# Reordering the learning step of a two-layer memory and mixture kernel

## The chip, the cores and the metric

The kernel is one program on one core of a Trainium2 chip. The metric is the device time of one execution in microseconds (us), as the median of several runs; one further execution was recorded by the hardware profiler, and its trace is what is read below. The engines are named as in the profile: PE is the matrix engine, PEld its weight loads, DVE the vector engine, ACT the scalar engine, POOL the GpSimd engine and SP the engine that issues DMAs.

## The reference, cut to what matters

The whole program is a chain of five parts on an input of 16 batches of 512 rows with 128 features. The change touches only the first part up to its end: a small memory network (`mem`: two weight matrices `w0`, `w1` and a scale `ln`) that is trained by gradient steps, one after the other, over 8 chunks of 64 rows of all 16 batches.

```python
def mem_fwd(params, x):
    w0, w1, ln = params
    h = jax.nn.silu(x @ w0.T)
    y = h @ w1.T
    return x + rmsnorm(y, ln)
...
k = rmsnorm(jax.nn.silu(xc @ wk_w.T), k_norm_w)
v = jax.nn.silu(xc @ wv_w.T)
...
def step(carry, inp):
    mem, surp = carry
    k_c, v_c, th_c, eta_c, beta_c = inp
    def loss_fn(p):
        pred = mem_fwd(p, k_c)
        return jnp.mean((v_c - pred) ** 2 * th_c[:, :, None])
    grads = jax.grad(loss_fn)(mem)
    total = jnp.sqrt(sum((jnp.sum(g * g) for g in grads)))
    clip = jax.lax.stop_gradient(jnp.minimum(MAX_GRAD_NORM / (total + 1e-06), 1.0))
    new_surp = tuple((eta_c * s_ - g * clip for s_, g in zip(surp, grads)))
    new_mem = tuple((beta_c * m + ns for m, ns in zip(mem, new_surp)))
    return ((new_mem, new_surp), None)
```

Chunk s+1 needs the weights that chunk s leaves, so the 8 steps are serial. Keys, values and the three gates of a chunk do not depend on the weights and are prepared ahead. After the steps come attention, a mixture of experts, a second attention and a second mixture; they are the same in both kernels.

## The kernel before, in words

`learn` is the first part. The 1024 rows of a chunk are held as 8 tiles (`CT`) of 128 rows and 128 features, in two halves of 4 tiles (`HT`), h = 0 and h = 1. Every engine has its own instruction list, written out by hand as a loop `for s in range(NC)` over the 8 steps; the order of the calls in that list is the order of execution on that engine, and semaphores (`Signal`, with `wait_ge` and `then_inc`) tie the lists together. There is no scheduler. One engine's waiting instruction holds up all that stand behind it in its list.

In step s the engines do two things at once.

The training step itself, along the data: PE multiplies keys by `w0` (`hidden`, L437), ACT takes a tanh (L629), DVE makes the hidden values from it (L858), PE transposes them (L451), ACT copies (L637), PE multiplies by `w1` (`output`, L461), ACT squares (L645), DVE sums (L868), POOL takes the root `r` (L768), ACT normalises (`normalise_y`, L651). DVE forms the error and its derivatives (`errors` L874 and L876, `derivatives` L881 to L890), which give per row a number `dr`; ACT multiplies by it (`along_y`, L657), DVE subtracts and so has the gradient `dy` of a half (`remainder`, L895). PE transposes it (`transpose_dy`, L469), ACT copies the transpose (`copy_dyt`, L667), PE sends it back through `w1` (`grad_hidden`, L478), DVE multiplies it by the slope of the silu (`grad_hidden`, L904; the slope itself is made before by ACT in `less_two`, L641, and DVE in `slope`, L862), and PE sums the gradients of `w1` (`grad_w1`, L491), `ln` (`grad_ln`, L487) and `w0` (`grad_w0`, L498). Then come their norm (PE L505 to L508, ACT L671 to L678), the clipping factor (DVE L908 to L912, POOL L772) and the new weights (`update`, L914 to L918).

The preparation of later chunks, in between: `project(s+2)` (PE L397) multiplies the rows of chunk s+2 by the key and the value weights, half 1 first; its half 0 writes banks 4 and 5, which the transposed keys of chunk s+1 (PE L406) hold until ACT has copied them out (`copy_kt`, L611). ACT takes tanh of the projections (`project_tanh`, L587), DVE makes silu of them (`silu`, L836). The tanh form of silu leaves twice the value, so ACT halves the values of a chunk (`halve_v`, L598), and POOL subtracts them from the keys (`subtract_v`, L787). ACT squares the keys (`square_k`, L592) and scales them (`scale_k`, L603). For chunk s+3 ACT normalises the input (`normalise_x`, L567) and PE transposes it (L382); for chunk s+4 DVE takes the statistics of the input (`statistics`, L825 and L830). `keep_surprise` (ACT L663) scales the old momentum, which only `decayed` (DVE L899) and the update read.

## Time and profile before

| what | value |
|---|---|
| median of 3 runs | 3584.17 us (3581.29 to 3584.71) |
| profiled execution | 3609.93 us |
| its span, first to last instruction | 3608.1 us |
| PE busy | 3255.2 us, 90% of the span |
| DVE busy | 2575.5 us, 71% |
| ACT busy | 2079.1 us, 58% |
| POOL busy | 838.7 us, 23% |
| mean granted PE clock | 0.960 of full speed |

The profiled execution is 25.8 us longer than the median, so differences are taken inside the trace and then carried to the median. "Granted clock" is 1.00 at 2.4 GHz and 0.50 at 1.2 GHz. The first weights are used at 51.63 us, and the last update ends at 381.73 us; the eight steps between them are the stretch that the change touches. A busy share over the whole span says little about them, since it is mostly made by the four parts behind.

### The profile page before, as it was taken

The numbers are of one execution on the slowest core, as the hardware profiler recorded it, in microseconds if no ns is written. First come the engines' busy times: TensorE is split into PE (matmuls) and PEld (weight loads), VectorE is DVE, ScalarE is ACT, GpSimd is POOL, SyncE is SP. The second block draws the span as 40 slices with busy tenths as digits, with TensorE's granted clock in tenths as the row PEclk, the third lists the DMA queues.
The fourth block names the chain that finished last, engine by engine and source line by source line (L and its number), as shares of the span: only waits on it lengthen the run. The fifth ranks groups of instructions, "written<-read, shape, count | busy, mean of one in ns | idle before, by whom it ended". The sixth has DMA issues, their size and how long they took to land. (4 is left out here: it accounts for less than half of the span.)

```text
span 3608.1 us, 77385 instructions
## 1 busy us (share of the span) xinstructions
PE 3255.2 (90%) x30347; PEld 1894.3 (53%) x30347; DVE 2575.5 (71%) x5104; ACT 2079.1 (58%) x4212; POOL 838.7 (23%) x753
## 2 busy tenths in 40 slices
PE   6887599999999699999999999769999999999998
PEld 5776322222222277777777777535555444444454
DVE  5776688888888266676666776577777777777774
ACT  6664177777777544434334333226667776777766
POOL 3331111101110132422423323133333121112110
PEclk8998699999999899999999999879999999999999
DMA  4100211111110000110110110032222112111101
GB/s 137 30 13 1 54 51 49 42 54 46 54 51 28 27 18 28 32 34 22 32 34 22 32 34 22 28 82 57 59 59 49 50 50 67 38 47 42 54 26 29
DMA packets 180473, 151.89 MB, mean 42 GB/s; under 512 B 44388, under 2 KB 160900, under 8 KB 179972
## 3 DMA queue, kind: packets, MB, share of 16 engines
q1 hardware_dynamic: 172228, 140.43, 13.8%
q0 software_dynamic: 6144, 4.72, 1.0%
q8 instruction: 257, 4.21, 0.5%
q10 hardware_dynamic: 1728, 1.57, 0.2%
q14 instruction: 116, 0.95, 0.1%
HBM read 48.45 MB, written 32.65 MB: 22 GB/s over the span
## 5 line engine op out<-in xcount | busy, mean ns | idle before, releaser
L1395 DVE TENSOR_REDUCE b_maxima<-psum 128x2 f32<-128x1024 f32 (+3 forms) x768 | 774.2, 1044 | 236.9 <-PE psum L1227 209.8
L1333 ACT ACTIVATE b_prob<-psum 128x512 f32<-128x512 f32 (+2 forms) x1536 | 725.5, 526 | 332.6 <-PE psum L1260 313.1
L1395 DVE TENSOR_REDUCE c_maxima<-psum 128x2 f32<-128x1024 f32 x512 | 602.6, 1221 | 119.3 <-PE psum L1221 118.2
L1333 ACT ACTIVATE c_prob<-psum 128x512 f32<-128x512 f32 x1024 | 535.9, 602 | 186.7 <-PE psum L1253 186.3
L1860 PEld LDWEIGHTS psum<-consts_layer,a_hid 128*128 128x128 f32 x4096 | 476.2, 192 | 53.6 <-issue 53.3
L1860 PE MATMUL psum<-consts_layer,a_hid 128*128 128x128 f32 x4096 | 477.8, 274 | 0.0
L1850 PE MATMUL psum<-a_x1t,consts_layer 128*128 128x512 f32 x1024 | 461.2, 596 | 11.6 <-issue 11.3
L1917 ACT ACTIVATE a_hid<-psum,consts_layer 128x512 f32<-128x512 f32 x512 | 347.9, 687 | 208.0 <-PE psum L1850 201.1
L1253 PE MATMUL psum<-b_qa,b_ka 64*128 64x512 bf16 (+3 forms) x2048 | 365.5, 303 | 60.8 <-ACT b_prob L1333 56.6
L1275 PE MATMUL psum<-b_prob,b_v 128*32 128x512 f32 (+3 forms) x4096 | 386.8, 450 | 0.3
L2062 DVE SCALAR_TENSOR_TENSOR a_acc<-psum,a_gprob,a_acc 128x128 f32<-128x128 f32 x512 | 143.8, 343 | 266.7 <-PE psum L1860 253.4
L1253 PE MATMUL psum<-c_qa,c_ka 64*128 64x512 bf16 x1024 | 271.0, 382 | 63.9 <-ACT c_prob L1333 62.4
L1221 PE MATMUL psum<-b_ka,b_qa 62*128 62x512 bf16 (+3 forms) x2048 | 300.1, 307 | 27.3 <-DMA b_ka<-b_part 13.2
L1850 PEld LDWEIGHTS psum<-a_x1t,consts_layer 128*128 128x128 f32 x1024 | 187.9, 191 | 213.1 <-issue 204.2
L1253 PEld LDWEIGHTS psum<-b_qa,b_ka 64*128 64x128 bf16 x2048 | 123.0, 93 | 297.5 <-ACT b_prob L1333 223.9
L1275 PE MATMUL psum<-c_prob,c_v 128*32 128x512 f32 x2048 | 272.7, 605 | 0.1
L1260 PE MATMUL psum<-b_kmask,b_pick 64*128 64x64 bf16 x4096 | 253.0, 191 | 0.0
L1221 PE MATMUL psum<-c_ka,c_qa 62*128 62x512 bf16 x1024 | 202.0, 392 | 27.4 <-DMA c_ka<-c_part 13.8
L1227 PE MATMUL psum<-b_qmask,b_pick 64*128 64x64 bf16 x4096 | 221.1, 191 | 3.3 <-issue 3.3
L1227 PEld LDWEIGHTS psum<-b_qmask,b_pick 64*128 64x128 bf16 x4096 | 194.4, 97 | 54.4 <-issue 7.3
L1260 PEld LDWEIGHTS psum<-b_kmask,b_pick 64*128 64x128 bf16 x4096 | 184.8, 95 | 47.3 <-issue 1.7
L1946 POOL TENSOR_TENSOR a_share<-a_gprob,consts_layer 128x512 f32<-128x512 f32 x128 | 134.1, 1048 | 273.2 <-DVE a_gprob L2001 264.4
(343 smaller groups left out, 4303.2 us busy)
## 6 DMA issues: line engine op xcount, KB each, us to landing
b_qa<-b_part SPq DMA_DIRECT2D x192, 128.0 KB
c_qa<-c_part SPq DMA_DIRECT2D x96, 128.0 KB, 2.5
c_ka<-c_part SPq DMA_DIRECT2D x90, 128.0 KB, 2.5
b_ka<-b_part SPq DMA_DIRECT2D x90, 128.0 KB
consts_layer<-layer_in SPq DMA_DIRECT2D x1, 5419.0 KB, 19.2
m_xin<-x SPq DMA_DIRECT2D x16, 256.0 KB, 4.2
xnt<-m_xt SPq DMA_DIRECT2D x16, 256.0 KB, 2.7
c_xt<-xnt SPq DMA_DIRECT2D x16, 256.0 KB, 2.8
```

Source lines behind the costliest of these rows:

```text
L1221: last = nc.tensor.matmul(out[:, half, k0:k0 + w], qa[rows, hh, t * P:(t + 1) * P], ka[rows, hh, 0:w], start=True, stop=not self.causal)
L1227: last = nc.tensor.matmul(out[:, half, k1:k1 + HALF], self.pick[n][rows, :], self.qmask[rows, :], start=False, stop=n == 1)
L1253: last = nc.tensor.matmul(outs[half][:, k0:k0 + w], ka[rows, hh, t * P:(t + 1) * P], qa[rows, hh, q0:S], start=True, stop=not self.causal)
L1260: last = nc.tensor.matmul(outs[half][:, k0 + n * HALF:k0 + (n + 1) * HALF], self.pick[n][rows, :], self.kmask[rows, :], start=False, stop= ...
L1275: last = nc.tensor.matmul(self.acc[32 * j:32 * (j + 1), q0:S], self.values(p)[:, t, column:column + 32], self.prob[:, s % 2, j, q0:S], sta ...
L1333: self.nc.scalar.activation(out, src, ACT.Exp, scale=SCALE).then_inc(self.s.free, 1)
L1395: self.nc.vector.reduce_max(out, src, X).then_inc(self.m.free, 1)
L1850: nc.tensor.matmul(bank[4 + u % 3], K("up0", e * F0 + f * P, P), x1t[n][:, :], start=True, stop=True).then_inc(up_ready.sem, 1)
L1860: last = nc.tensor.matmul(tiled(2 + e % 2)[:, t, :], hid[:, e % 2, f, t * P:(t + 1) * P], K("down0", (e * FC + f) * D, D), start=f == 0, s ...
L1917: nc.scalar.activation(hid[:, e % 2, f, :], bank[4 + u % 3], ACT.Relu, bias=K("upb0", u, 1)).then_inc(hid_ready.sem, 1)
L1946: own.done(nc.gpsimd.tensor_tensor(share[k % 2][:, :, :], along(gprob[n][:, :, k], D), over(K("downb0", k * D, D), T), ALU.mult))
L2062: last = nc.vector.scalar_tensor_tensor(acc[n][:, t, :], tiled(2 + e % 2)[:, t, :], gprob[n][:, t, e:e + 1], acc[n][:, t, :], ALU.mult, AL ...
```

## The change

Counts of instructions stay as they are, but for one: the eight halvings of the values (1 per chunk) go, and one halving of the value weights, done once at the start, stands in their place (`halve_wv`); the tanh of the values then takes scale 1.0. The rest is order.

- ACT: `copy_kt` goes ahead of `normalise_y(s, 1)`; `keep_surprise` goes behind `along_y(s, 0)`; `normalise_x(s+3)` is no longer split and stands behind `copy_dyt(s, 1)`; `square_k(s+2, 1)` goes ahead of `along_y(s, 1)`; `scale_k(s+2)` is split, half 0 ahead of `copy_xs`.
- PE: `grad_w1(s, 0)` goes ahead of `grad_hidden(s, 0)`; `project` waits for the halved weights also.
- DVE: `statistics(s+4)` is split in `sums`, now ahead of `hidden(s)`, and `moments`, ahead of the first slope; `slope(s, 1)` goes behind `grad_hidden(s, 0)`; `remainder(s, 0)` goes ahead of `errors(s, 1)`; `sum_products` goes behind `grad_hidden(s, 1)`.
- POOL: `subtract_v` waits for the silu, not for the halving.

```diff
@@ PE @@
                 def project(n, halves=(1, 0)):
                     for h in halves:
+                        pe.wait_ge(wv_halved.sem, 1)
                         pe.wait_ge(xt_copied.sem, xt_copied.at(n, h + 1))
...
                     transpose_dy(s, 0)
+                    grad_w1(s, 0)
                     grad_hidden(s, 0)
-                    grad_w1(s, 0)
                     grad_ln(s, 1)
@@ ACT @@
-                            nc.scalar.activation(to[:, part(h), :], tiles(bank[K_BANK[h][j]]), ACT.Tanh, scale=0.5).then_inc(proj_tanh.sem, 1)
+                            nc.scalar.activation(to[:, part(h), :], tiles(bank[K_BANK[h][j]]), ACT.Tanh, scale=(0.5, 1.0)[j]).then_inc(proj_tanh.sem, 1)
...
-                def halve_v(n):
-                    act.wait_ge(silu_ready.sem, silu_ready.at(n, 4))
-                    nc.scalar.activation(tv[n % 2][:, :, :], tv[n % 2][:, :, :], ACT.Copy, scale=0.5).then_inc(vn_ready.sem, 1)
+                def halve_wv():
+                    act.wait_ge(consts, 32)
+                    nc.scalar.activation(K("wv"), K("wv"), ACT.Copy, scale=0.5).then_inc(wv_halved.sem, 1)
...
                     normalise_y(s, 0)
-                    keep_surprise(s)
-                    normalise_y(s, 1)
                     if has(s + 1):
                         copy_kt(s + 1)
+                    normalise_y(s, 1)
                     if has(s + 2):
                         project_tanh(s + 2, (1,))
                     along_y(s, 0)
+                    keep_surprise(s)
                     if has(s + 2):
                         project_tanh(s + 2, (0,))
                     copy_dyt(s, 0)
-                    if has(s + 3):
-                        normalise_x(s + 3, (0,))
-                    if has(s + 1):
-                        halve_v(s + 1)
+                    if has(s + 2):
+                        square_k(s + 2, 1)
                     along_y(s, 1)
                     copy_dyt(s, 1)
                     if has(s + 3):
-                        normalise_x(s + 3, (1,))
+                        normalise_x(s + 3)
                     if has(s + 2):
-                        square_k(s + 2, 1)
                         square_k(s + 2, 0)
                     square_grads(s)
                     square_g0(s)
                     if has(s + 3):
                         for h in range(2):
                             copy_xt(s + 3, h)
+                    if has(s + 2):
+                        scale_k(s + 2, (0,))
+                    if has(s + 3):
                         copy_xs(s + 3)
                     if has(s + 2):
                         gate_tanh(s + 2)
-                        scale_k(s + 2)
+                        scale_k(s + 2, (1,))
@@ POOL @@
-                    pool.wait_ge(vn_ready.sem, vn_ready.at(n, 1))
+                    pool.wait_ge(silu_ready.sem, silu_ready.at(n, 4))
@@ DVE @@
                 for s in range(NC):
+                    if has(s + 4):
+                        sums(s + 4)
                     for h in range(2):
                         hidden(s, h)
                     if has(s + 1):
                         weigh_keys(s + 1)
                         gates(s + 1)
+                    if has(s + 4):
+                        moments(s + 4)
+                    slope(s, 0)
                     output_deviations(s)
                     errors(s, 0)
                     derivatives(s, 0)
                     if has(s + 2):
                         silu(s + 2, 1)
+                    remainder(s, 0)
                     errors(s, 1)
-                    remainder(s, 0)
                     derivatives(s, 1)
                     decayed(s)
                     remainder(s, 1)
                     if has(s + 2):
                         silu(s + 2, 0)
                     grad_hidden(s, 0)
+                    slope(s, 1)
+                    grad_hidden(s, 1)
                     if has(s + 2):
                         sum_products(s + 2)
-                    grad_hidden(s, 1)
-                    if has(s + 4):
-                        statistics(s + 4)
                     update(s)
```

On PE, in a middle step from the projection to the gradient of `w0`, before:

```order
L397 MATMUL psum<-consts_memory,m_xt 128x128 x16
L487 MATMUL psum<-m_en,m_ths 128x128 x4
L469 MATMUL psum<-consts_shared,m_dy 128x128 x4
L478 MATMUL psum<-mem,m_dyt 128x256 x4
L491 MATMUL psum<-m_hid,m_dy 128x256 x4
L487 MATMUL psum<-m_en,m_ths 128x128 x4
```

and with the change:

```order
L398 MATMUL psum<-consts_memory,m_xt 128x128 x16
L488 MATMUL psum<-m_en,m_ths 128x128 x4
L470 MATMUL psum<-consts_shared,m_dy 128x128 x4
L492 MATMUL psum<-m_hid,m_dy 128x256 x4
L479 MATMUL psum<-mem,m_dyt 128x256 x4
L488 MATMUL psum<-m_en,m_ths 128x128 x4
```

The gradient of `w1` (hidden values and `dy`) now stands between the transpose of `dy` and the product that needs its copy (`m_dyt`).

On DVE, in the middle of a step from the last derivative of half 0 on, before (`m_dn` and `m_p` are the parts of `dy`, `m_tk` and `m_tv` are the silus, `m_m` is the error of half 1):

```order
L890 TENSOR_TENSOR m_dn<-m_dn,m_rth 128x512
L836 SCALAR_TENSOR_TENSOR m_tk<-m_tk,psum 128x512
L836 SCALAR_TENSOR_TENSOR m_tv<-m_tv,psum 128x512
L874 TENSOR_TENSOR m_m<-m_nrm,mem 128x512
L876 TENSOR_TENSOR m_m<-m_m,m_kv 128x512
L895 TENSOR_TENSOR m_dy<-m_dn,m_p 128x512
```

and with the change:

```order
L893 TENSOR_TENSOR m_dn<-m_dn,m_rth 128x512
L840 SCALAR_TENSOR_TENSOR m_tk<-m_tk,psum 128x512
L840 SCALAR_TENSOR_TENSOR m_tv<-m_tv,psum 128x512
L898 TENSOR_TENSOR m_dy<-m_dn,m_p 128x512
L877 TENSOR_TENSOR m_m<-m_nrm,mem 128x512
L879 TENSOR_TENSOR m_m<-m_m,m_kv 128x512
```

The gradient `dy` of half 0 has moved ahead of the two instructions of the error of half 1.

On ACT, from the first normalisation to the second copy of the transposed gradient, before:

```order
L651 ACTIVATE m_nrm<-psum,m_r 128x128 x4
L663 ACTIVATE m_keep<-m_surp,m_eb 128x640
L651 ACTIVATE m_nrm<-psum,m_r 128x128 x4
L611 ACTIVATE m_kt<-psum 128x512 x2
L587 ACTIVATE m_tk<-psum 128x512
L587 ACTIVATE m_tv<-psum 128x512
L657 ACTIVATE m_p<-m_nrm,m_dr 128x128 x4
L587 ACTIVATE m_tk<-psum 128x512
L587 ACTIVATE m_tv<-psum 128x512
L667 ACTIVATE m_dyt<-psum 128x512
L567 ACTIVATE m_xn<-m_xin,m_shift,m_rstd 128x128 x4
L598 ACTIVATE m_tv<-m_tv 128x1024
```

and with the change:

```order
L651 ACTIVATE m_nrm<-psum,m_r 128x128 x4
L611 ACTIVATE m_kt<-psum 128x512 x2
L651 ACTIVATE m_nrm<-psum,m_r 128x128 x4
L585 ACTIVATE m_tk<-psum 128x512
L585 ACTIVATE m_tv<-psum 128x512
L657 ACTIVATE m_p<-m_nrm,m_dr 128x128 x4
L663 ACTIVATE m_keep<-m_surp,m_eb 128x640
L585 ACTIVATE m_tk<-psum 128x512
L585 ACTIVATE m_tv<-psum 128x512
L667 ACTIVATE m_dyt<-psum 128x512
L590 ACTIVATE m_sq,m_ks<-m_tk 128x128 x4
L657 ACTIVATE m_p<-m_nrm,m_dr 128x128 x4
```

The copy of the transposed keys (`m_kt`) has moved up two places, and where two groups (`m_xn` and the halving of `m_tv`) stood ahead of the second `along_y` there is one group of squares.

## Rows read from the trace of the kernel before

**Rows 1.** Busy time in the learning steps (start:end, length, each engine's busy us)

```profile
core 0: us, PE busy (x) PEld busy (x) DVE busy (x) ACT busy (x) POOL busy (x), PEclk, DMA share, GB/s
...
55.00:383.00 328.00, 262.32 (x1532) 232.71 (x1530) 226.59 (x442) 196.89 (x536) 82.74 (x71) 0.89 0.06 14
...
178.99:219.96 40.97, 34.98 (x215) 31.42 (x212) 30.55 (x65) 28.19 (x79) 13.29 (x13) 0.92 0.05 14
```

**Rows 2.** Timeline of PE, step 3: start, length, line, tiles, [idle <- releaser]

```profile
192.26 3.17 PE L397 MATMUL psum<-consts_memory,m_xt 128*128 128x128 f32 x16 [3.22 <-ACT m_kt L611]
195.22 1.59 PE L487 MATMUL psum<-m_en,m_ths 128*128 128x128 f32 x8
197.81 0.66 PE L469 MATMUL psum<-consts_shared,m_dy 128*128 128x128 f32 x4 [1.00 <-DVE m_dy L895]
199.15 3.24 PE L478 MATMUL psum<-mem,m_dyt 128*128 128x256 f32 x8 [0.69 <-ACT m_dyt L667]
202.19 2.37 PE L491 MATMUL psum<-m_hid,m_dy 128*128 128x256 f32 x8
...
205.28 0.60 PE L469 MATMUL psum<-consts_shared,m_dy 128*128 128x128 f32 x4
...
216.28 3.70 PE L437 MATMUL psum<-mem,m_kt 128*128 128x256 f32 x16
```

**Rows 3.** Timeline of DVE, step 3

```profile
186.13 1.22 DVE L862 SCALAR_TENSOR_TENSOR m_dz<-m_tz,m_dz 128x1024 f32<-128x1024 f32 x1
...
195.02 0.68 DVE L836 SCALAR_TENSOR_TENSOR m_tv<-m_tv,psum 128x512 f32<-128x512 f32 x1
195.62 0.68 DVE L874 TENSOR_TENSOR m_m<-m_nrm,mem 128x512 f32<-128x512 f32 x1
...
197.06 0.69 DVE L895 TENSOR_TENSOR m_dy<-m_dn,m_p 128x512 f32<-128x512 f32 x1
...
200.38 0.16 DVE L889 TENSOR_TENSOR m_dr<-m_dot,m_rth 128x4 f32<-128x4 f32 x1
...
201.18 0.89 DVE L899 SCALAR_TENSOR_TENSOR m_base<-mem,m_eb,m_keep 128x640 f32<-128x640 f32 x1
202.77 0.69 DVE L895 TENSOR_TENSOR m_dy<-m_dn,m_p 128x512 f32<-128x512 f32 x1 [0.70 <-ACT m_p L657]
...
209.38 1.22 DVE L904 SCALAR_TENSOR_TENSOR m_dz<-m_dz,psum 128x1024 f32<-128x1024 f32 x1 [2.19 <-PE psum L478]
...
219.96 2.35 DVE L858 SCALAR_TENSOR_TENSOR m_hid<-m_tz,psum 128x1024 f32<-128x1024 f32 x2 [2.67 <-ACT m_tz L629]
```

**Rows 4.** Timeline of ACT, step 3

```profile
189.28 0.84 ACT L663 ACTIVATE m_keep<-m_surp,m_eb 128x640 f32<-128x640 f32 x1
...
190.99 1.13 ACT L611 ACTIVATE m_kt<-psum 128x512 f32<-128x512 f32 x2
...
193.81 1.28 ACT L657 ACTIVATE m_p<-m_nrm,m_dr 128x128 f32<-128x128 f32 x4 [0.72 <-DVE m_dr L889]
...
201.48 1.26 ACT L657 ACTIVATE m_p<-m_nrm,m_dr 128x128 f32<-128x128 f32 x4
...
216.58 2.44 ACT L603 ACTIVATE m_tk<-m_tk,m_krstd 128x128 f32<-128x128 f32 x8
```

**Rows 5.** Timeline of POOL, step 3

```profile
186.16 3.09 POOL L768 TENSOR_TENSOR m_r<-m_ss,m_power 128x4 f32<-128x4 f32 x2 [5.07 <-DVE m_ss L869]
```

**Rows 6.** Busy time and granted clock (PEclk) in three stretches

```profile
199.75:203.10 3.35, 3.35 (x10) 2.61 (x9) 2.58 (x5) 2.99 (x8) 0.00 (x0) 0.50 0.01 2
203.20:220.20 17.00, 17.00 (x103) 15.27 (x101) 10.32 (x32) 10.73 (x43) 8.44 (x9) 1.00 0.12 32
73.30:80.10 6.80, 5.57 (x15) 4.27 (x16) 5.53 (x11) 4.25 (x10) 0.05 (x1) 0.51 0.00 0
```

**Rows 7.** Timeline of ACT, step 6

```profile
317.69 1.28 ACT L657 ACTIVATE m_p<-m_nrm,m_dr 128x128 f32<-128x128 f32 x4 [1.69 <-DVE m_dr L889]
```

**Rows 8.** Timeline of DVE, step 6

```profile
319.74 0.69 DVE L895 TENSOR_TENSOR m_dy<-m_dn,m_p 128x512 f32<-128x512 f32 x1
```

More of the change, by code:

```diff
@@ L557, in _, with normalise_x @@
             def _(act):
-                def normalise_x(n, halves=(0, 1)):
-                    if 0 in halves:
-                        act.wait_ge(rstd_ready.sem, rstd_ready.at(n, 1))
-                    if 0 in halves and n > 0:
+                def normalise_x(n):
+                    act.wait_ge(rstd_ready.sem, rstd_ready.at(n, 1))
+                    if n > 0:
                         act.wait_ge(xt_ready.sem, xt_ready.at(n, 0))
@@ L564, in normalise_x @@
                         act.wait_ge(prod_ready.sem, prod_ready.at(n - 1, 1))
-                    for h in halves:
-                        for t in range(h * HT, (h + 1) * HT):
-                            last = nc.scalar.activation(xn[:, t, :], xin[n % 2][:, t, :], ACT.Identity, bias=shift[:, t:t + 1], scale=rstd[:, t:t + 1])
-                    if 1 in halves:
-                        last.then_inc(xn_ready.sem, 1)
+                    for t in range(CT):
+                        last = nc.scalar.activation(xn[:, t, :], xin[n % 2][:, t, :], ACT.Identity, bias=shift[:, t:t + 1], scale=rstd[:, t:t + 1])
+                    last.then_inc(xn_ready.sem, 1)
                 def copy_xt(n, h):
@@ L820, in _, with sums @@
                 own = OwnSteps(ctx0, nc, "m_own", dve)
-                def statistics(n):
+                def sums(n):
                     dve.wait_ge(x_loaded[n % 2].sem, x_loaded[n % 2].at(n // 2, 2))
+                    if n > 0:
+                        dve.wait_ge(stats_ready.sem, stats_ready.at(n, 0))
                     for t in range(CT):
@@ L918, in update @@
                     nc.vector.scalar_tensor_tensor(surp[:, INTER:M], bank[7][:, 0:INTER + D], clip, keep[:, INTER:M], ALU.mult, ALU.add).then_inc(surp_ready.sem, 1)
-                statistics(0)
+                sums(0)
+                moments(0)
                 dve.wait_ge(consts, 32)
@@ L925, in _ @@
                 nc.vector.sem_inc(mem_ready.sem, 1)
-                statistics(1)
+                sums(1)
+                moments(1)
                 for h in (1, 0):
                     silu(0, h)
-                statistics(2)
+                sums(2)
+                moments(2)
                 weigh_keys(0)
@@ L935, in _ @@
                 sum_products(1)
-                statistics(3)
+                sums(3)
+                moments(3)
                 for s in range(NC):
+                    if has(s + 4):
+                        sums(s + 4)
                     for h in range(2):
```

16 lines of the change are left out of this document (9 added, 7 removed).

## The prediction, made before the changed kernel was run

> **What bounds the kernel now.** I read the stages first. The eight learning steps lie between 55 and 383 us, with no engine full: PE is busy for 262 of 328 us, DVE for 227, ACT for 197 [rows 1]. So the steps are a chain of waits, not one full engine, and one middle step (178.99 to 219.96, 40.97 us) shows it: PE 34.98 us busy, DVE 30.55, ACT 28.19 [rows 1]. Steps 1 to 4 all have this length and step 3 stands for them.
>
> Then I followed the chain through step 3 on the timelines. From `hidden` to the normalised outputs it goes around all engines, and the edits barely touch it. From there DVE works almost without a break: error and derivatives of half 0, silus of the next projection, error of half 1, and only then `dy` of half 0, at 197.06 [rows 3]. PE has by then waited twice: 3.22 us for the copy of the transposed keys, before the second half of the projection, and 1.00 us for this `dy` [rows 2]. It transposes `dy`, waits another 0.69 us for ACT's copy, and from 199.15 on is never idle up to 220.2: the backward products, the gradients, the transposes of the input, the next `hidden` [rows 2], with 17.00 of 17.00 us busy from 203.2 to 220.2 [rows 6]. Therefore the step is bound by DVE up to the first `dy`, and by PE behind it. The second `dy` shows that it is not bound by DVE there: it starts at 202.77 and ends at 203.46, and PE transposes it only at 205.28 [rows 2, 3], so that it lies 1.8 us ready.
>
> The clock is the second part of the picture. Between 199.75 and 203.10 the granted clock is 0.50, that is 1.2 instead of 2.4 GHz, in a PE that had just waited 1.00 and 0.69 us [rows 2, 6]. The eight multiplications of `grad_hidden` take 3.24 us in it, and those of `grad_w1` 2.37 [rows 2].
>
> **The edits on the path.** `remainder(s, 0)` ahead of `errors(s, 1)`. The silus leave DVE free for the next instruction at 195.62, where the first of the two instructions of the error stood [rows 3]. The new occupant needs `along_y(s, 0)`, which ACT ends at 193.81 + 1.28 = 195.09 [rows 4]. So `dy` of half 0 starts at 195.62 instead of 197.06: 1.44 us gained. It still comes behind the silus on DVE, so nothing shorter than that is to be had.
>
> `grad_w1(s, 0)` ahead of `grad_hidden(s, 0)`. It needs only `dy` and the hidden values, so it runs while ACT copies the transpose; the 0.69 us of idleness go. Together PE comes to the second transpose 1.44 + 0.69 = 2.13 us earlier, at 203.15, if the clock is as slow for as long as before.
>
> The second `dy` must keep up with that. Its ACT part ran at 201.48, behind half a normalisation and the halving of the values; its `dr` was made by 200.38 + 0.16 = 200.54 [rows 3, 4]. With both out of the way, and the squares that take their place done long before, `along_y` runs from 200.58 to 201.84. On DVE `decayed` starts at 201.18 and takes 0.89, the next can start at about 201.98 [rows 3]. So this `dy` runs from 201.98 to 202.67, and the transpose may start at 202.72. That is the floor: 205.28 - 202.72 = 2.56 us per step is the most that can be had, and 2.13 lies inside it.
>
> Behind the transpose the work of PE is unchanged and full. One wait could open in it: the second `grad_hidden` on DVE (1.22 us) must be ready for the second half of the `w0` gradient. Before, it started at 209.38 on the heels of PE [rows 3]. Now DVE has one more piece there, the slope of half 1, 1.22 us [rows 3]. After the first `grad_hidden` (it comes at about 203.8: `dy` at 201.98, then three starts 0.60 apart) it is done at about 206.2, and PE has its product at 209.3 - 2.1 = 207.2. It fits with 1 us to spare; without that cover it would cost what is over.
>
> **The edits off the path, all at nothing.** `copy_kt` forward takes the place of `keep_surprise` at 189.28, instead of 190.99 [rows 4]: its copies end at 189.28 + 1.13 = 190.4, and PE, idle since 192.26 - 3.22 = 189.04, waits 1.4 us instead of 3.22. But it then ends its projection and `grad_ln` earlier, between 192.8 (both at full clock) and 195.2 (both at half, as now), and waits for `dy`, which comes from DVE at 196.3. It is a wait moved, not one removed. Bounds: 0, or with a faster clock part of the half-speed stretch (up to 1.7 us). `keep_surprise` (0.84 us) then stands in an ACT that waits for the transpose at 196.4 at the earliest, while its reader `decayed` comes at 201.18. The second normalisation slips by 0.3 us; its reader stands more than 4 us behind. `scale_k` in halves frees ACT before the next tanh (before, the 2.44 us from 216.58 ran until the tanh at 218.9 [rows 4]), up to 0.7 us for tanh of half 0. But PE delivers `hidden` of half 1 only at 216.28 + 3.70 = 219.98 [rows 2], the tanh of half 1 hangs on this, and PE takes the transposes in order: 0 to 0.1 us. The statistics leave DVE ahead of the update, where it waited for the norm anyway; `sums` (1.6 us) go into the 2.67 us in which DVE waits for the tanh [rows 3], some 0.3 us of it left when the tanh comes 0.7 earlier. Without that cover they would cost what is over, in four steps only (s = 0 to 3), and up to about 1 us once in step 0, where the input they read may land late. The whole normalisation of the input behind the second copy, with the squares, fills ACT until about a microsecond before the `w0` gradient is ready. The halving of the weights (a 128x128 piece, once) stands at the start beside POOL's work on the first deviations: 0 to 0.4 us. On POOL the subtraction still waits for the second `dy` and starts earlier with it; the two instructions behind it, the key deviations and the root, come earlier or as before. The further wait on PE is long fulfilled.
>
> One rule speaks against a moved piece. The slope of half 1 reads two tiles from memory and now falls near the end of POOL's subtraction. In the trace such a slope ran beside POOL's root from 186.13 in 1.22 us, POOL being busy from 186.16 to 189.25 [rows 3, 5], and was not stretched. The Trainium skill (GPSIMD Engine Reference, section 8, Key points) says that GpSimd shares its memory interfaces with VectorE and that they contend when the DVE instruction has two SBUF inputs. By that rule the slope would be stretched; if it were doubled, the 1 us of spare would be overdrawn by some 0.2 us a step, 2 us in all. By the row it is nothing, and the row decides.
>
> **The last two steps.** Steps 6 and 7 have no projection, so no silus stand before `dy`. In step 6 `along_y` ends at 317.69 + 1.28 = 318.97 [rows 7], DVE now waits for it, and `dy` starts at 319.0 instead of 319.74 [rows 8]: 0.74, with the 0.69 of the copy 1.43 us. DVE pays for it by coming to the second `dy` 0.7 us later. If that lay ready by no more than the 1.8 us of step 3, then 1.43 + 0.7 would overdraw it by 0.3 us; I take it as covered. Step 7 has the same pattern.
>
> **The sum.** Steps 0 to 5: 6 x 2.13 = 12.8. Steps 6 and 7: 2 x 1.43 = 2.9. Together 15.7 us. The profiled execution of 3609.9 would become 3594.2; taken from the median, 3584.2 - 15.7 = 3568.5, and I say 3568. The four parts behind are the same and start earlier by the same amount.
>
> **Rivals.**
> First, the clock pays out in full. If PE is at 1.00 more of the time it is held only by the floor: 6 x 2.56 + 2.9 = 18.3, in step 0, where 6.80 us at 0.51 were paid [rows 6], perhaps 1 more: 3565. For it: the wait of 3.22 us is halved. Against: a wait of up to 3.5 us for `dy` arises instead.
>
> Second, the clock takes back. A fall as long as that of step 0 (6.8 us at half speed, 3.4 lost) in every step costs 1.7 us more than the 3.35 us of now [rows 6]. Then PE comes to the second transpose at 204.85, and 0.4 us a step are left: 6 x 0.4 + 2.9 = 5.3, 3579. For it: the single wait is longer. Against: from `dy` on there is no wait left in which to stay slow.
>
> Third, slower. PE now can run dry before the second `dy`, for up to 1.5 us if it was fast until then. If this makes the clock fall behind it, in the 17 us that are full and at 1.00 now [rows 6], each microsecond at half clock costs half of one, all of it on the path. It decides from 4.3 us at half clock per step, which eat the 2.13. With the 6.8 of step 0 [rows 6] it is 3.4 - 2.13 = 1.3 a step, 8 steps 10 us: 3594. For it: the clock fell after waits of 1.00 and 0.69. Against: such a dry spell only arises when PE was fast, and the full stretch behind it is long.
>
> Fourth, the change doesn't reach the end: DVE is held in `sums` by the input load, or the next part starts on a transfer that isn't earlier. Then 0 to 7 us are gained: 3580. For it: nothing but the moved read. Against: the rows of DVE show no wait for a load in these steps [rows 3], and the read moves forward by less than a quarter of a step.
>
> **How the numbers follow.** The forecast (2.13 a step, 3563 to 3574 with a clock that varies by a microsecond a step) 0.58; all to the floor or beyond, 3558 to 3565, 0.17; clock takes back 0.13; slower 0.05; does not reach the end 0.07. What this kernel's measurement can tell from no change is 0.2%, 7.2 us, so 3577 is the line. Above it lie the slower case, the fourth case (same) and a third of the second: faster 0.84, same 0.11, slower 0.05. The range 3559 to 3578 leaves out about 1.5 in 10.
>
> **What would show it.** A middle step of 38.5 to 39.2 us instead of 40.97; `dy` of half 0 directly behind the silus; no idle PE before `grad_hidden(s, 0)`; a wait of 1 to 3.5 us before the first transpose of `dy` and 1.4 before the second half of the projection; the second transpose on the heels of the second `dy`, within 0.5 us. I am wrong if that transpose lies where PE is still late by over 1 us, if `sums` delay the hidden values, or if PEclk is 0.50 anywhere in the stretch behind the second transpose.

## The result: 27 us less, where 15.7 were forecast

| kernel | median, us | runs |
|---|---|---|
| before | 3584.44 | 4 (3581.29 to 3585.27) |
| changed | 3557.4 | 4 (3552.92 to 3559.65) |

The ratio is 0.9925, with a 95% interval from 0.9907 to 0.9942. The sign was right, but the time lies below the range of 3559 to 3578. The profiled execution took 3552.92 us.

The learning steps over the whole stretch, in one middle step (`hidden` of step 2 to `hidden` of step 3), and behind that step's second `dy`, as in [rows 1, 6]:

```profile
core 0: us, PE busy (x) PEld busy (x) DVE busy (x) ACT busy (x) POOL busy (x), PEclk, DMA share, GB/s
50.73:351.63 300.90, 245.38 (x1545) 220.78 (x1545) 228.69 (x453) 194.01 (x537) 78.44 (x75) 0.95 0.06 15
126.34:163.48 37.14, 31.32 (x215) 28.56 (x214) 30.41 (x66) 27.49 (x79) 12.23 (x12) 1.00 0.12 29
152.40:163.40 11.00, 10.97 (x70) 10.10 (x70) 7.71 (x13) 8.43 (x31) 4.83 (x4) 1.00 0.33 75
```

A step takes 37.14 us instead of 40.97, and the clock is granted in full all through it. PE in this step, to be read beside [rows 2]:

```profile
140.23 2.02 PE L398 MATMUL psum<-consts_memory,m_xt 128*128 128x128 f32 x16 [0.49 <-ACT m_kt L611]
142.09 1.06 PE L488 MATMUL psum<-m_en,m_ths 128*128 128x128 f32 x8
146.06 0.66 PE L470 MATMUL psum<-consts_shared,m_dy 128*128 128x128 f32 x4 [2.91 <-DVE m_dy L898]
146.55 1.89 PE L492 MATMUL psum<-m_hid,m_dy 128*128 128x256 f32 x8
148.28 1.89 PE L479 MATMUL psum<-mem,m_dyt 128*128 128x256 f32 x8
...
152.43 0.66 PE L470 MATMUL psum<-consts_shared,m_dy 128*128 128x128 f32 x4 [1.36 <-DVE m_dy L898]
...
163.48 3.70 PE L438 MATMUL psum<-mem,m_kt 128*128 128x256 f32 x16
```

DVE [rows 3] and POOL [rows 5] in the same step:

```profile
144.72 0.68 DVE L840 SCALAR_TENSOR_TENSOR m_tv<-m_tv,psum 128x512 f32<-128x512 f32 x1
145.32 0.68 DVE L898 TENSOR_TENSOR m_dy<-m_dn,m_p 128x512 f32<-128x512 f32 x1
...
151.69 0.68 DVE L898 TENSOR_TENSOR m_dy<-m_dn,m_p 128x512 f32<-128x512 f32 x1
...
154.62 1.29 DVE L866 SCALAR_TENSOR_TENSOR m_dz<-m_tz,m_dz 128x1024 f32<-128x1024 f32 x1
156.58 1.22 DVE L907 SCALAR_TENSOR_TENSOR m_dz<-m_dz,psum 128x1024 f32<-128x1024 f32 x1 [0.68 <-PE psum L479]
```

```profile
136.93 1.01 POOL L768 TENSOR_TENSOR m_r<-m_ss,m_power 128x4 f32<-128x4 f32 x1 [4.80 <-DVE m_ss L872]
138.72 1.01 POOL L768 TENSOR_TENSOR m_r<-m_ss,m_power 128x4 f32<-128x4 f32 x1 [0.78 <-DVE m_ss L872]
```

The order on PE and DVE is as drawn, and the second transpose follows the end of the second `dy` at 152.37 by 0.06 us. The surprise stands on POOL: the two roots took 3.09 us together beside the slope [rows 5], the first of them 2.07, and now take 1.01 each, alone. Counted from the start of `hidden`, the first transpose of `dy` comes at 19.72 us instead of 22.50, and the second at 26.09 instead of 29.97.

In four of the eight steps the clock is still at half speed for a stretch at or behind the first `dy` (a slow stretch, in what follows): 6 and 7, and 0 and 3, which take 38.48 and 38.43 us. Here is step 3, behind the same wait of 2.91 us:

```profile
183.19 1.11 PE L470 MATMUL psum<-consts_shared,m_dy 128*128 128x128 f32 x4 [2.91 <-DVE m_dy L898]
184.10 3.62 PE L492 MATMUL psum<-m_hid,m_dy 128*128 128x256 f32 x8
187.51 2.67 PE L479 MATMUL psum<-mem,m_dyt 128*128 128x256 f32 x8
```

### The profile page after: what moved, and what is told of

Its sections match the earlier page's. It is cut to its first block and busy times, and to the rows that moved or that the text cites. A ratio compares the mean times of both kernels' runs of the same rounds, so it can differ in the third digit from the quotient of the medians.

```text
span 3551.1 us, 77379 instructions
## 1 busy us (share of the span) xinstructions
PE 3219.4 (91%) x30347; PEld 1869.3 (53%) x30347; DVE 2574.3 (72%) x5104; ACT 2074.0 (58%) x4205; POOL 829.8 (23%) x753
## 5 line engine op out<-in xcount | busy, mean ns | idle before, releaser
L1861 PE MATMUL psum<-a_x1t,consts_layer 128*128 128x512 f32 x1024 | 461.3, 596 | 10.5 <-issue 10.2
```

What stands on the lines that cost most here:

```text
L1861: nc.tensor.matmul(bank[4 + u % 3], K("up0", e * F0 + f * P, P), x1t[n][:, :], start=True, stop=True).then_inc(up_ready.sem, 1)
```

## The experiments

All runs together. "End" is the start of the last transposes of the learning part in the trace, the next two are the starts of the two transposes of `dy` in step 2 (before: step 3), from the step's start of `hidden`. e1 to e4, e5 to e8, e9 to e12 and e13 with e14 each shared their own runs of the kernel before.

| kernel | end, us | 1st dy | 2nd dy | step | median, us | ratio, interval |
|---|---|---|---|---|---|---|
| before | 381.88 | 22.50 | 29.97 | 40.97 | 3584.4 | 1 |
| changed | 351.63 | 19.72 | 26.09 | 37.14 | 3557.4 | 0.9925 (0.9907 to 0.9942) |
| e1 before, again | 379.24 | 22.52 | 30.00 | 40.99 | 3581.6, one run | |
| e2 before + slope moved | 381.03 | 21.43 | 29.95 | 40.95 | 3582.4 | 0.9995 (0.9983 to 1.0008) |
| e4 before + both orders of dy | 365.11 | 21.26 | 27.43 | 38.48 | 3568.3 | 0.9961 (0.9948 to 0.9974) |
| e3 changed, slope back | 362.57 | 20.78 | 27.18 | 38.20 | 3567.6 | 0.9959 (0.9946 to 0.9972) |
| e5 changed + two inputs | 361.21 | 20.62 | 27.15 | 38.15 | 3571.0 | 0.9962 (0.9951 to 0.9973) |
| e6 changed + one input | 352.36 | 19.72 | 26.09 | 37.14 | 3562.3 | 0.9940 (0.9922 to 0.9957) |
| e7 before + filler | 363.09 | 22.50 | 28.29 | 39.29 | 3568.7 | 0.9958 (0.9944 to 0.9972) |
| e8 e2 + filler | 356.72 | 21.44 | 27.23 | 38.70 | 3561.7 | 0.9941 (0.9926 to 0.9956) |
| e9 changed + filler | 350.13 | 19.73 | 26.09 | 37.15 | 3555.8 | 0.9925 (0.9908 to 0.9942) |
| e10 changed, dr early | 353.96 | 19.96 | 26.46 | 37.46 | 3557.4 | 0.9928 (0.9911 to 0.9944) |
| e11 e9 and e10 | 347.49 | 19.96 | 25.84 | 36.89 | 3550.0 | 0.9909 (0.9892 to 0.9925) |
| e12 changed, both orders back | 380.31 | 21.17 | 29.97 | 40.96 | 3587.8 | 1.0014 (1.0003 to 1.0025) |
| e13 changed, only PE's back | 364.34 | 19.71 | 28.53 | 39.53 | 3568.5 | 0.9956 (0.9940 to 0.9973) |
| e14 changed, only DVE's back | 366.90 | 21.18 | 28.68 | 39.68 | 3574.8 | 0.9972 (0.9961 to 0.9983) |

What follows the end took 3199.5 us in the changed kernel, 3200.5 in e1 and 3211.2 in e12, with the other experiments between (span minus end). That scatter of up to 12 us lies outside the edits, so mechanisms are read from the steps, and medians only confirm them.

**e1, the kernel before once more.**

> The kernel before, unchanged, for a second trace. If the 25.8 us by which its first profiled execution stood above the median were the cost of profiling, this one stands as far above (3610). If they were a disturbance in the fourth part, this one lies near 3584, with the learning steps as long as before: 330.2 us from the first product of hidden to the last transpose of w1, 40.97 us for a middle step.

It took 3581.56 us, with the same middle steps. The 25 us by which the profiled execution before stood above its median belong to that one execution and do not come from profiling: they lie behind the learning part, where it took 3226.2 us against 3200.5. Within the learning part only step 0 differs (39.18 instead of 41.73). Its slow stretch lies ahead of the first `dy` here, and behind it in the trace before (73.30 to 80.10 [rows 6]):

```profile
67.40:74.20 6.80, 5.84 (x26) 5.58 (x27) 6.63 (x13) 4.07 (x10) 0.00 (x0) 0.50 0.00 0
```

Comparisons use e1: the changed kernel gains 379.24 - 351.63 = 27.6 us in the learning steps, which is the whole result.

**e2, the slope alone, on the kernel before.**

```diff
+                    slope(s, 0)
                     for h in range(2):
-                        slope(s, h)
...
                     grad_hidden(s, 0)
+                    slope(s, 1)
```

> The kernel before with one edit: the slope of half 1 goes behind the first grad_hidden on DVE. By the theory formed after the result, that the slope (two SBUF inputs) stretches POOL's root of half 0 from 1.01 to 2.06 us, the root falls to about 1.0, everything behind comes 1.05 us earlier in each step, and the time falls by 8 x 1.05 = 8.4 us to 3576. By the theory of the prediction, that the slope is not on the path, nothing changes: 3584, and the root keeps its 2.06.

POOL and PE in step 2:

```profile
145.11 1.01 POOL L768 TENSOR_TENSOR m_r<-m_ss,m_power 128x4 f32<-128x4 f32 x1 [5.08 <-DVE m_ss L869]
```

```profile
155.69 1.12 PE L469 MATMUL psum<-consts_shared,m_dy 128*128 128x128 f32 x4 [2.50 <-DVE m_dy L895]
157.49 3.78 PE L478 MATMUL psum<-mem,m_dyt 128*128 128x256 f32 x8 [0.69 <-ACT m_dyt L667]
161.07 2.42 PE L491 MATMUL psum<-m_hid,m_dy 128*128 128x256 f32 x8
...
164.21 0.60 PE L469 MATMUL psum<-consts_shared,m_dy 128*128 128x128 f32 x4
```

The root falls to 1.01 and the first `dy` comes 1.07 us earlier, yet the second transpose does not move (29.95) and nor does the time. The clock took it back: the three pieces behind the wait last 1.12 + 3.78 + 2.42 = 7.32 us, against 0.66 + 3.24 + 2.37 = 6.27 in [rows 2], which is 1.05 more. The granted clock of a step of the kernel before (two stretches of step 3), then of e2, shows where that comes from:

```profile
192.95:196.30 3.35, 3.35 (x18) 3.35 (x18) 3.28 (x6) 2.40 (x7) 0.00 (x0) 0.50 0.00 0
199.75:203.10 3.35, 3.35 (x10) 2.61 (x9) 2.58 (x5) 2.99 (x8) 0.00 (x0) 0.50 0.01 2
```

```profile
155.35:162.07 6.72, 5.69 (x15) 4.40 (x16) 5.45 (x11) 4.24 (x10) 0.18 (x1) 0.50 0.01 2
```

Before, half of the slow time lay ahead of the first `dy`, over the projection and `grad_ln`, where PE had to wait anyway. In e2 a step has about as much slow time, but nearly all of it behind the first `dy`, where it costs.

**e3, the changed kernel with the slope back between the two sums of squares.**

```diff
                     for h in range(2):
+                        if h == 1:
+                            slope(s, 1)
...
-                    slope(s, 1)
```

> The changed kernel with the slope of half 1 back between the two sums of squares. Port theory: the root of half 0 takes 2.06 us again, and since dy of both halves hangs on it, a step is 1.05 us longer: 3557.4 + 8.4 = 3566. Theory of the prediction: no difference, 3557, or a little less, since DVE has 1.2 us less to do between the two grad_hidden.

```profile
138.83 3.08 POOL L768 TENSOR_TENSOR m_r<-m_ss,m_power 128x4 f32<-128x4 f32 x2 [4.80 <-DVE m_ss L874]
```

The roots are long again (3.08 us), the first `dy` comes 1.06 us later than in the changed kernel, and the time is 3567.6 us, 0.4 us from the forecast. So everything that the forecast priced is in this kernel, and what it missed is the slope: 10.2 us by the medians, 10.9 by the ends. The slow stretch behind the first `dy` is here as long as before (step 2):

```profile
148.85:152.20 3.35, 3.18 (x10) 2.73 (x11) 3.28 (x7) 2.35 (x11) 0.00 (x0) 0.50 0.00 0
```

In step 3 it is about twice as long, and that step takes 39.54 us instead of 38.20 to 38.30.

**e4, the two orders of `dy` alone, on the kernel before.**

```diff
+                    grad_w1(s, 0)
                     grad_hidden(s, 0)
-                    grad_w1(s, 0)
...
+                    remainder(s, 0)
                     errors(s, 1)
-                    remainder(s, 0)
```

> The kernel before with two edits alone: remainder of half 0 ahead of the errors of half 1 on DVE, grad_w1 of half 0 ahead of grad_hidden of half 0 on PE. Theory of the prediction: PE comes 2.13 us earlier to the second transpose, but the second dy stays at 203.46, so at most 205.28 - 203.52 = 1.76 us a step in steps 0 to 5 and 1.43 in the last two: 13.4 us, 3571. Rival: the clock takes part back, the half-speed stretch grows and less than 1 us a step is left: above 3577.

The step falls to 38.48 us, 2.5 less, where the expectation allowed at most 1.76: the second `dy` does not stay where it was. PE has its slow stretch ahead of the first `dy`, comes to it without a wait, and then waits for the second at full clock:

```profile
156.64 0.66 PE L469 MATMUL psum<-consts_shared,m_dy 128*128 128x128 f32 x4 [1.22 <-DVE m_dy L895]
```

This start, 27.42 us into the step, is the forecast's floor (29.97 - 2.56 = 27.41). The rival, that the clock leaves less than 1 us a step, falls. The other edits together (projection, halved weights, statistics) add 0.2 to 0.3 us a step to this: e3's second `dy` stands at 27.18 instead of 27.43.

**e5 and e6, the cause of the long root.** One instruction is added to the changed kernel where the slope had stood; nobody reads its result. Both forms take the same time on DVE. They differ in the number of tiles that they read, and also in what they write (1024 columns against 4).

```diff
                     for h in range(2):
+                        if h == 1:
+                            # e5: two inputs in SBUF
+                            nc.vector.scalar_tensor_tensor(extra[:, :, :], tz[:, part(1), :], -1.0, hid[:, part(1), :], ALU.add, ALU.mult)
+                            # e6, in its place: one input
+                            nc.vector.tensor_reduce(extra[:, :], hid[:, part(1), :], X, ALU.add)
```

> The changed kernel with one added VectorE instruction between the two statistics sums of half 1, whose two inputs both lie in SBUF and whose result nobody reads; it stands where slope(s,1) stood before. Theory 'two inputs in SBUF hold POOL up': POOL's root (L768, 128x4) goes back from 1.01 us to about 2.06 for the first of the two, the normalised outputs come about 1 us later in each of eight steps, the step goes from 37.13 to about 38.2 and the kernel to about 3566 us, although VectorE itself does not delay anything (it waited 0.58 us there). Rival 'the root was long because of something else in the old order': root stays at 1.01 and the time within 2 us of 3557.

> The same place, but the added VectorE instruction is a sum over half 1 of the hidden layer: one input in SBUF, about as long, result not read. Theory 'two inputs': the root stays at 1.01 us and the kernel at 3557 +- 3 us, unless the sum is so long that it delays the moments on VectorE. Rival 'any VectorE work beside POOL stretches POOL': root again about 2.06 and the kernel about 3566 us as with two inputs.

DVE's added instruction and POOL's roots, first e5, then e6:

```profile
138.03 1.22 DVE L872 SCALAR_TENSOR_TENSOR m_extra<-m_tz,m_hid 128x1024 f32<-128x1024 f32 x1
...
138.19 2.93 POOL L769 TENSOR_TENSOR m_r<-m_ss,m_power 128x4 f32<-128x4 f32 x2 [4.81 <-DVE m_ss L875]
```

```profile
137.46 1.21 DVE L872 TENSOR_REDUCE m_extra<-m_hid 128x4 f32<-128x1024 f32 x1
...
137.63 1.01 POOL L769 TENSOR_TENSOR m_r<-m_ss,m_power 128x4 f32<-128x4 f32 x1 [4.81 <-DVE m_ss L875]
139.54 1.01 POOL L769 TENSOR_TENSOR m_r<-m_ss,m_power 128x4 f32<-128x4 f32 x1 [0.91 <-DVE m_ss L875]
```

The two instructions are equally long and at the same place. Beside the one with two inputs in SBUF the first root takes 2.93 - 1.01 = 1.92 us, and the step goes to 38.15; beside the one with one input it takes 1.01, and the step stays 37.14, to the hundredth. DVE's own instruction is not longer in either. e5 and e6, measured together, lie 8.6 us apart by the medians and 8.85 by the ends. e5's median is 5 us above the 3566 that were expected. e6's is 5 us above the changed kernel's, its learning steps only 0.7: the rest is within the scatter named above.

That it is the second input, and not the larger output, other traces settle. POOL's small addition for the key norm (`m_kvar`, 128x8) stands beside an instruction of DVE that writes 128x1024 both in step 5 of the changed kernel (shown first) and in step 2 of e8, the kernel of the next group (shown second). In the changed kernel DVE reads two tiles in SBUF, in e8 one in SBUF and one in PSUM:

```profile
267.67 1.04 POOL L763 TENSOR_SCALAR m_kvar<-m_ks 128x8 f32<-128x8 f32 x1
...
267.32 1.29 DVE L866 SCALAR_TENSOR_TENSOR m_dz<-m_tz,m_dz 128x1024 f32<-128x1024 f32 x1
```

```profile
160.91 0.24 POOL L775 TENSOR_SCALAR m_kvar<-m_ks 128x8 f32<-128x8 f32 x1 [2.86 <-ACT m_sq L604]
...
160.45 1.21 DVE L916 SCALAR_TENSOR_TENSOR m_dz<-m_dz,psum 128x1024 f32<-128x1024 f32 x1
```

The addition takes 1.04 us beside the two inputs in SBUF and 0.24 beside the one. In all these cases DVE had started first. DVE can pay too, where POOL has started first. This is step 6 of the changed kernel:

```profile
301.46 2.36 POOL L787 TENSOR_TENSOR m_kv<-m_kn,m_tv 128x1024 f32<-128x1024 f32 x1 [12.37 <-DVE m_dy L898]
...
302.43 2.47 DVE L866 SCALAR_TENSOR_TENSOR m_dz<-m_tz,m_dz 128x1024 f32<-128x1024 f32 x1
```

The moved slope takes 2.47 us instead of 1.22, and costs nothing only because DVE then still waits 0.69 us for PE. So the contention is real, it needs the second input in SBUF, and where one pays in these rows, it is the instruction that started later. At the place of the slope before, that was the root.

**e7 and e8, the clock on the kernel before.** Small matmuls of constants into an unused part of a bank fill PE's waits.

```diff
+                def fill(n, b=6):
+                    for _ in range(n):
+                        nc.tensor.matmul(bank[b][:, 256:384], K("ident"), K("ones"), start=True, stop=True)
...
                     grad_ln(s, 0)
+                    fill(10)
                     transpose_dy(s, 0)
+                    fill(2)
```

> The kernel before, with small matmuls of constants into an unused part of a bank in TensorE's waits of the learning step (12 ahead of the first project of half 0, 10 behind grad_ln(s,0), 2 in the copy's gap, others in the last steps); nobody reads them. Theory 'the half-speed stretch pins the step': the granted clock stays 1.00 through the step, the step goes from 40.97 to about 39.2 us (T_dy1 at the floor set by the second dy, 1.76 us earlier), the kernel from 3583 to about 3570 us. Rival 'the step is set by the chain of VectorE, POOL and ScalarE alone': the clock rises, the step stays within 0.3 us of 40.97 and the time within 3 us. Rival 'filler gets in the way': slower than 3585.

> The kernel before with slope(s,1) moved behind grad_hidden(s,0), and the same added matmuls. Alone the moved slope gave nothing (ratio 0.9995). Theory 'the half-speed stretch pins the step': with the clock kept up the 1.06 us that POOL's root loses now comes through: the step is about 1.05 us shorter than with the added matmuls alone (about 38.1 us), the kernel about 8 us faster than with them alone. Rival 'the moved slope needs the new order of dy': no more than 2 us between the two.

PE in step 2 of e7, then of e8, where it waits for DVE's `dz` near the end:

```profile
153.91 2.00 PE L480 MATMUL psum<-mem,m_dyt 128*128 128x256 f32 x8 [0.24 <-ACT m_dyt L679]
```

```profile
155.72 0.60 PE L471 MATMUL psum<-consts_shared,m_dy 128*128 128x128 f32 x4
...
161.71 1.99 PE L500 MATMUL psum<-m_dz,m_kn 128*128 128x256 f32 x8 [0.20 <-DVE m_dz L916]
```

With no reordering at all, e7 brings 1.68 us a step by full clock in front of the second `dy`, close to the 1.76 expected; the rivals (no change, or slower) fall. On top of it the slope move now does pay: the second `dy` comes 28.29 - 27.23 = 1.06 us earlier. But only 39.29 - 38.70 = 0.59 reach the step, so the expected 8 us became 7.0. In e8 both the slope (1.29 us) and the sum of products (1.47 us) stand in DVE ahead of the second gradient of the hidden values, which starts at 160.45, and PE waits for it (0.20 us, and the products behind are no longer in one piece). In the order of the changed kernel, where the sum of products stands behind that gradient, the cover holds (DVE waits 0.68 for PE at 156.58).

**e12, e13 and e14, which order opens the step.** The changed kernel with both orders of `dy` undone, only PE's, or only DVE's; the lines are those of e4, backward.

> The changed kernel with the two orders that the forecast priced undone: errors(s,1) stands ahead of remainder(s,0) again and grad_hidden(s,0) ahead of grad_w1(s,0); slope, halved weights, projection and statistics stay as changed. Alone on the kernel before the moved slope gave nothing (steps of 40.95 us). Theory 'a half-speed stretch ahead of the second dy pins the step, only the order of dy opens it': steps 40.5 to 41.0 us, the kernel at 3578 to 3585 us. Rival 'the rest of the change is worth its 1.32 us a step by itself': steps about 39.6 us, the kernel at about 3573 us.

> The changed kernel with one order undone: grad_hidden(s,0) stands ahead of grad_w1(s,0) again, so TensorE waits 0.69 us more for ScalarE's copy behind the first transposes of dy; remainder(s,0) stays ahead of errors(s,1). Theory 'the copy's wait on top of the wait for dy is what lets the clock fall in every step': granted clock 0.50 behind the first dy in every step, steps of 38.5 us or more (up to the 40.96 of the other pinned kernels), kernel 3566 to 3584 us. Rival 'with dy early the second dy sets the step anyway': steps 37.1 to 37.8 us, kernel 3557 to 3563 us.

> The changed kernel with the other order undone: errors(s,1) stands ahead of remainder(s,0) again, so the first dy comes 1.44 us later, as the forecast priced it, and the second at the same time or 0.7 us sooner; grad_w1(s,0) stays ahead of grad_hidden(s,0). Theory 'only where TensorE has its work in one piece behind dy the step opens': T_dy0 at 21.2 us from the start of hidden instead of 19.7, a wait of 4.4 us before it, the clock falls to 0.50 behind it, steps 38.5 to 39.5 us, kernel 3568 to 3576 us. Rival 'pinned unless both orders are there': steps 40.9 to 41.0 us, kernel 3580 to 3588 us.

PE in step 2 of e12, then of e14:

```profile
157.11 0.66 PE L470 MATMUL psum<-consts_shared,m_dy 128*128 128x128 f32 x4 [4.37 <-DVE m_dy L898]
158.45 3.78 PE L479 MATMUL psum<-mem,m_dyt 128*128 128x256 f32 x8 [0.69 <-ACT m_dyt L667]
162.03 3.16 PE L492 MATMUL psum<-m_hid,m_dy 128*128 128x256 f32 x8
```

```profile
151.60 1.12 PE L470 MATMUL psum<-consts_shared,m_dy 128*128 128x128 f32 x4 [4.36 <-DVE m_dy L898]
152.51 3.62 PE L492 MATMUL psum<-m_hid,m_dy 128*128 128x256 f32 x8
155.92 2.45 PE L479 MATMUL psum<-mem,m_dyt 128*128 128x256 f32 x8
```

Without both orders the step is 40.96 us, although the first `dy` comes 1.33 us earlier than before: the three pieces take 0.66 + 3.78 + 3.16 = 7.60 us, 1.33 more than before, and nearly all of it is at half speed:

```profile
157.80:164.55 6.75, 6.10 (x14) 4.88 (x15) 6.64 (x12) 3.04 (x13) 2.37 (x1) 0.50 0.01 2
```

That earlier work gives no time in this order (the "pin" of the expectations) is confirmed, though the median lies 3 us above what was expected. Each order alone opens about half: steps 1 to 4 take 38.13 to 39.53 us in e13 and 38.42 to 39.78 in e14. Both rivals fall, "the second dy sets the step anyway" and "pinned unless both orders are there". The clock fell in every step of e13, as its theory said, but three of these four steps are shorter than its 38.5 us; e14's theory held, but for 0.1 and 0.3 us at the ends of its range of steps.

**e9, e10 and e11, a better version.** e9 puts filler into the changed kernel. e10 moves the product `dn` behind the small product `dr` (it still stands ahead of `dy`) and the decayed memory down to the update, and e11 does both.

```diff
-                    nc.vector.tensor_tensor(dn[:, a, :], m[:, a, :], wide_ln, ALU.mult)
...
+                    own.done(nc.vector.tensor_tensor(dn[:, a, :], m[:, a, :], wide_ln, ALU.mult))
...
-                    decayed(s)
...
                         sum_products(s + 2)
+                    decayed(s)
                     update(s)
```

> The changed kernel with small matmuls of constants, read by nobody, in TensorE's waits (behind grad_ln(s,0) and grad_ln(s,1), and in the last steps). In the changed kernel's trace steps 0 and 3 are 38.48 and 38.43 us long with a half-speed stretch, the others without one 37.13, and the last step's first products run at half speed (5.34 us). Theory 'with the wait closed the second dy sets the step at full clock': steps 0 and 3 fall to about 37.2, the undisturbed steps stay within 0.1 us of 37.13, the kernel is 3 to 6 us faster than the changed one. Rival 'the clock still pins all steps': the undisturbed ones get shorter too, over 8 us in all. Rival 'filler gets in the way': each step 0.2 us longer or more.

> The changed kernel with two VectorE instructions taken out of the chain that ends in dy: the product dn (128x512, 0.60 us to the next start) goes behind the small product dr, and the decayed memory (0.81 us) behind the sum of products ahead of the update. Theory 'VectorE's chain to the second dy sets the step, and TensorE waits 1.36 us for it': T_dy1 0.7 to 1.3 us earlier, the step 36.0 to 36.5 instead of 37.13, the kernel 5 to 9 us faster than the changed one, unless the longer chain behind dz takes it back. Rival 'the decayed memory is late for the update': TensorE and the normalisation wait for the update instead, the step within 0.3 us of 37.13.

> Both of the last two edits on the changed kernel. If both theories hold, the clock stays 1.00 through all steps, every step is 36.0 to 36.5 us long, and the kernel takes about 3546 us, 10 to 12 less than the changed one; if the clock's stretches and the chain hide one another, no more than the better of the two alone.

PE in step 2 of e10, then of e11 (L505 is the filler):

```profile
147.59 1.12 PE L470 MATMUL psum<-consts_shared,m_dy 128*128 128x128 f32 x4 [3.16 <-DVE m_dy L898]
148.50 3.14 PE L492 MATMUL psum<-m_hid,m_dy 128*128 128x256 f32 x8
```

```profile
144.70 2.40 PE L505 MATMUL psum<-consts_shared 128*128 128x128 f32 x20
148.02 0.66 PE L470 MATMUL psum<-consts_shared,m_dy 128*128 128x128 f32 x4 [0.93 <-DVE m_dy L909]
148.52 1.89 PE L492 MATMUL psum<-m_hid,m_dy 128*128 128x256 f32 x8
```

e9 evens out step 3 (37.13 instead of 38.43) and leaves the full-clock ones at 37.14 and 37.15, but step 0 (38.81) met a slow stretch in its first products; the end moves by 1.5 us only, and the medians differ by 1.6 where 3 to 6 were expected. e10 fails: the first `dy` comes 0.24 us later (20.0 instead of 19.7), since at two more places an instruction now directly follows the one whose result it reads (their starts lie 0.72 us apart, those of independent ones 0.60), PE waits 3.16 instead of 2.91 us, and the clock falls in every step. With both, the clock holds, the second `dy` comes 0.25 us earlier, and the steps take 36.89: not the 36.0 to 36.5 hoped for, but 4.1 us less at the end and 3550.0 us in all (3546.0 to 3551.66, where 3546 was expected). That is below every run of the changed kernel (from 3552.92), though the two were not measured together, and the intervals of their ratios overlap. It is the best version here, by the steps; by the medians its lead over the changed kernel is not shown.

## Why the prediction was wrong, step by step

**The step that failed: the slope at nothing.** The prediction read DVE's row, saw a slope of 1.22 us that was not stretched beside POOL's root, and concluded "By the row it is nothing, and the row decides"; of the root it said that it comes "earlier or as before". The other row of the same pair showed the price: two roots of the same shape in 3.09 us, of which one ran beside the slope and one after it. The rule of the Trainium skill (GPSIMD Engine Reference, section 8, Key points), contention when the DVE instruction has two SBUF inputs, was the right one, and the root agrees with it (2.07 us beside the slope, 1.01 without), but it was weighed for the moved slope alone. Its size here is 1.06 us a root, on the path in each of eight steps: 8.5 us (e3, e5, e6). By the ends it is 10.9: in steps 1 to 5 the changed kernel is shorter than e3 by 1.07 to 1.17 each, in step 7 by 1.03, and in step 6 by 3.59, since e3 has more slow time there (39.90 instead of 36.31 us). What lies ahead of step 1 brings another 0.7.

What the prediction feared of the moved slope happened once: it was doubled in step 6 (2.47 us), and its cover held. In steps 0 to 5 it began 0.2 us before POOL's subtraction ended and took 1.28 to 1.29 us.

**The orders of `dy`: right in direction, near in size by luck.** 1.44 + 0.69 us a step was the working. The 1.44 is confirmed: e13 and e14 differ from the changed kernel in the first `dy` by 0.00 and 1.46 us. The 0.69 shows as the wait for the copy that is gone, but what it pays by itself depends on the clock and was not isolated. The sum of 15.7 us met 16.7 (379.24 to 362.57, e3), and 3568 met 3567.6. That is closer than the working deserves. In steps 1, 2, 4 and 5 e3 gives 2.7 to 2.8 us, above the floor of 2.56 (by the 0.26 below), where 2.13 were priced. Step 3, with its longer slow stretch, gives 1.4, and step 0, which was short in e1 already, 0.9. The first rival (the clock pays out to the floor) is what happened in the undisturbed steps.

**The floor.** 22.50 + 7.47 = 29.97 was the second transpose before. The floor lay 2.56 below it, and e4, with the two orders alone, stands on it; the changed kernel lies 3.88 below. The difference of 1.32 is the root (1.06) and an earlier tanh (0.26). The prediction held that from `hidden` to the normalised outputs the edits barely touch the chain, and gave the halved `scale_k` 0 to 0.1 us. It was 0.26, seen as 21.43 against 21.17 between e2 and e12, which differ by the edits other than the slope's and the two orders. In these two traces the tanh of half 0 starts 2.64 and 2.01 us into the step, behind eight scalings (2.44 us) and behind four (1.27 us), and the first sum of squares is ready 0.27 us earlier. The split of `scale_k` was not run alone.

**The clock.** "As slow for as long as before" held in e3 for five of the first six steps (step 3 had about twice as much). In steps 1, 2, 4 and 5 of the changed kernel the slow stretch is absent. Where the two orders are missing, it covers nearly all of the work behind the first `dy`, and 1.07 and 1.33 us of earlier first `dy` were given back in full (e2, e12). So the gains do not add: the slope is worth 0 us alone, 0.6 a step with filler, and 1.1 to 1.2 on top of the orders. The sum of terms had no place for that.

**What held.** The wait for the key copy was put at 1.4 us and was 1.56 with the long root (e3). PE ran dry before the second `dy`, and behind it the clock stayed at 1.00 in steps 0 to 5 (in step 2 with 10.97 of 11.00 us busy), so the slower rival did not come. The sign that it named, a clock of 0.50 behind the second transpose, shows only at the end of the part: from the last 0.1 us of step 6 through most of the first products of step 7 (5.34 us instead of 3.70; 5.38 before), and at the end of step 7. The sums did not delay `hidden`, and the second gradient of the hidden values kept its cover. The fourth rival fell too: the gain arrived in full at the end.

## What to carry to other kernels

When two engines overlap, read the rows of both: the one you are pricing may be fine while its neighbour pays. Where one paid in these traces, it was the one that had started later, so a move can turn the roles. A group of two instructions of one shape whose sum is not twice one of them is the sign. Ask of each term of a sum what clock it assumes: where a slow stretch comes to lie over the work that was brought forward, a gain gives nothing until the order or the waits around it change. Test edits in pairs: here 0 and 14 us alone, with 2.5 for the remaining edits, made 27.6.

## What the hardware showed beyond that

POOL's small root (128x4) took 1.01 us alone and 2.07 beside a 128x1024 instruction of DVE with two SBUF inputs that had started 0.03 us before it, 1.01 beside one of the same length with one. DVE's instruction took 1.22 and 1.21 us. The other way round, the same instruction of DVE took 2.47 us where it started 0.97 us behind a 128x1024 subtraction of POOL, and ended 1.08 us after it. Not every overlap costs: the second root of the changed kernel (138.72) and the instruction of the error (128x512, two SBUF inputs) that DVE started 0.43 us behind it took 1.01 and 0.69 us, as elsewhere.

The same wait of 2.91 us before the first transpose left the granted clock at 1.00 in steps 1, 2, 4 and 5 of the changed kernel and not in 0 and 3; in e3 it fell in each of these six, and behind a wait of 3.16 also (e10). Three kernels whose first `dy` came at 22.50, 21.43 and 21.17 us had the second transpose at 29.97, 29.95 and 29.97. In the kernel before, the slow stretch behind the first `dy` begins 24.4 us into each of steps 1 to 5; in e3 it begins 22.1, 21.3, 20.6 and 19.9 us into steps 0 to 3. So the length of the wait does not decide alone, and when it falls may count as well; no run here tests that. Why the slow stretch takes back exactly what was gained is not settled by these runs.
